# A third PSUM bank for the MLP's first layer and the dense step of a Swin-style block kernel

## The chip, the cores and the metric

The kernel runs on one core of a Trainium2 chip. The metric is the time of one execution on the device in microseconds (us); less is better. TensorE is PE in the rows (its weight loads are PEld), VectorE is DVE, ScalarE is ACT, GpSimd is POOL and SyncE, which issues most transfers, is SP.

## The reference, cut to what matters

The input is 8 images of 16 channels and 56 x 56 pixels. A depthwise 9 x 9 convolution makes 144 channels of it, which with the 16 of the input are 160 per pixel. Two Swin blocks follow, the second with windows shifted by 3 pixels, then a dense step to 144 channels, a second depthwise convolution that sums 9 channels into one, and a 1 x 1 convolution.

```python
for i, (shift, mask) in enumerate(zip(SHIFTS, (None, MASK1))):
    # inside: x = ln1(x); qkv = xw @ qkvw + qkvb; softmax(q k^T * s + bias + mask) @ v; out @ projw + projb
    #         x = sc + x; h = ln2(x); h = gelu(h @ w1 + b1) @ w2 + b2; return x + h
    x3 = _swin_block(x3, shift, mask, ln1g[i], ..., w1[i], b1[i], w2[i], b2[i])
x3 = x3 @ linw + linb
```

Windows are 7 x 7 = 49 pixels, there are 5 heads of 32, and the hidden layer of the MLP has 640 = 5 x 128 columns. Everything is in fp32; large products are made of four passes over operands that are split in a high part, a low part and a rest.

## The kernel before, in words

There are three phases. `phase_a` makes the first convolution and prepares weights, `phase_c` makes the second one. Between them, and most of the time, `phase_b` walks over 64 strips: a strip is two rows of windows' worth of tokens (14 image rows, 784 tokens, held as 7 tiles t of 112), 32 strips in layer 0 and 32 in layer 1. The loop is software-pipelined: `body(i, la, lm, ln)` holds the attention of strip i (layer `la`), the MLP of strip i-1 (layer `lm`), and the first norm, queries, keys and values of strip i+1 (`ln`). In layer 1 it also holds the dense step of strip i-1 (`linear`, with the 1 x 1 convolution folded in). Each engine has its own instruction stream, written out by hand in the order of its `body`, and waits on semaphores at constants or at values worked out from the loop variable; nothing reorders the work, so the order in the code is the order on the engine.

The eight PSUM banks of `phase_b` are: `ra` (3, a ring for all products of the attention), `so` (2, scores and outputs of heads), `rm` (2) and `pt_ps` (1). `pt_ps` holds the attention weights turned by TensorE (`weights_turned`, L1493), four times a strip, and ScalarE copies it out (`weights_out`, L1092). Between the copy of the strip's fourth group and the first group of the next strip it is empty.

The two `rm` banks are taken in strict alternation, by the class `Ring`, by these uses of a body in this order:
- G0 to G9: the first layer of the MLP, `mlp_in` (L1526). Each is one block of 128 hidden columns for the first half of the strip (G0 to G4: 4 tiles, 448 columns of tokens) or the second (G5 to G9: 3 tiles, 336 columns), and has four matmuls: z2t_hi with w_hi, z2t_lo with w_hi, z2t_hi with w_lo, z2t_rest with w_rest, all on line L127 of a helper. ScalarE empties each with a GELU into `ht` (L1119).
- W0 to W5: the second layer (`mlp_out`, L1536, matmuls on L1543), emptied by VectorE (L1323).
- in layer 1 L0 to L3: the dense step (`linear`, L1557; 2, 2, 2 and 1 tiles of four matmuls), emptied by VectorE with one L1286 per tile, in the same order.
- T2A0 and T2C0: the first half of the next strip's second norm, turned by TensorE (`mlp_turned`, L1569, transposes on L1430). ScalarE rounds them into `z2t` (L1110) and VectorE takes the low parts (`t_lo`, L1302, L1309). With that the banks are free.

On TensorE the order around them is: G0 G1 G2, the turned second half (T2A1, T2C1, into `ra`), G3 G4, scores of group 1, G5 to G9, W0, scores of group 2, `front_turned(0)` (L1448: the next strip's first norm turned, which waits for GpSimd's `z1`, L987), `weights_turned(0)`, W1, and so on; at the end of a layer 1 body values of group 2, scores of the next strip's group 0, L0 to L3, T2A0, T2C0, values of group 3, B1, and the next body's G0. G0 reads `z2t`, so it waits until VectorE's `t_lo` has freed T2C0 (`t2_half_freed`, L839).

On VectorE the end of a layer 1 body is: normalise the first half (L1205), statistics of the last tiles (L1182), the seven L1286 of L0 to L3, the variance of the second half (L1193 to L1201), `t_lo` (two L1309), normalise the second half. Each semaphore of a bank counts how often it was filled (`rm_full`) or freed (`rm_free`). With strict alternation both banks have the same number of uses in a body, 9 in layer 0 and 11 in layer 1, and `m_before` multiplies that by the bodies done.

Of the kernel before, what the change touches and what calls it, by code (L numbers as in the profile page):

```python
# [23 lines left out]
B, C, H, W = 8, 16, 56, 56  # L24
# [30 lines left out]
FT = MLP // 128  # L55
# [34 lines left out]
def reach(engine, sem, value):  # L90

    if isinstance(value, int) and value <= 0:
        return
    engine.wait_ge(sem, value)


class Ring:


    def __init__(self, uses, banks, readers):  # L100
        self.uses, self.banks = uses, banks
        self.at = {u: n for n, u in enumerate(uses)}
        self.weight = [readers.get(u, 1) for u in uses]

    def slot(self, use):
        return self.at[use] % self.banks

    def filled(self, use):
        return self.at[use] // self.banks + 1
# [7 lines left out]

    def frees(self, slot):
        return sum(self.weight[slot::self.banks])


def split_passes(nc, out, hi, lo, rest, w_hi, w_lo, w_rest, act_moves):
# [8 lines left out]
def build(nc, x, f_ana, f_syn, ln1g, ln1b, qkvw, qkvb, projw, projb, rel, ln2g, ln2b, w1, b1, w2, b2,  # L131
          linwT, linb, convwT, convb, wmask, out):
    xs0 = nc.dram_tensor("xs0", [B, H, W, DIM], F32, kind="Internal")
    xs1 = nc.dram_tensor("xs1", [B, HP, HP, DIM], F32, kind="Internal")
    ys = nc.dram_tensor("ys", [B, H, YW, DIM], F32, kind="Internal")
    relT = nc.dram_tensor("relT", [WT, 2 * HEADS * WT], F32, kind="Internal")
    with ExitStack() as ctx:
        keep = Persistent(nc, ctx)
        late = Handed(nc, ctx, xs0, ys, f_syn)
        phase_a(nc, keep, late, x, f_ana, ln1g, ln1b, qkvw, qkvb, projw, projb, rel, relT, ln2g, ln2b, w1, b1,  # L140
                w2, b2, linwT, linb, convwT, convb, wmask, xs0)
        phase_b(nc, keep, late, xs0, xs1, ys)
        late.strips.close()
        phase_c(nc, keep, late, out)
# [562 lines left out]
def phase_b(nc, keep, late, xs0, xs1, ys):  # L707
    with ExitStack() as ctx:
# [3 lines left out]
        def sem(name):  # L712
            return ctx.enter_context(nc.semaphore(name))

        def bank(name):
            return ctx.enter_context(nc.psum_tensor(name, [128, 512], F32))

        ra = [bank(f"ra{n}") for n in range(3)]
        rm = [bank(f"rm{n}") for n in range(2)]
        so = ctx.enter_context(nc.psum_tensor("so", [128, 2 * 512], F32))  # L720
        pt_ps = bank("pt_ps")
# [31 lines left out]
        s_init, s_clear = sem("b_init"), sem("b_clear")  # L753
        ra_full = [sem(f"ra_full{n}") for n in range(3)]
        ra_free = [sem(f"ra_free{n}") for n in range(3)]
        rm_full = [sem(f"rm_full{n}") for n in range(2)]
        rm_free = [sem(f"rm_free{n}") for n in range(2)]
        s_st = [sem("stats1"), sem("stats2")]
        s_rs = [sem("rs1"), sem("rs2")]
        s_pow = sem("pow2")  # L760
# [12 lines left out]
        END = Ring(["OT0", "OT1", "OT2", "OT3", "P0", "P1", "P2", "T2A1", "T2C1"], 3, {})  # L773
        PAIRS = [(0, 2), (2, 1), (3, 1), (4, 1), (5, 1), (6, 1)]
        LPAIRS = [(0, 2), (2, 2), (4, 2), (6, 1)]
        T2 = ["T2A0", "T2C0"]
        MLP_USES = [f"G{g}" for g in range(2 * FT)] + [f"W{n}" for n in range(len(PAIRS))]
        LIN_USES = ["L0", "L1", "L2", "L3"]
        RM0 = Ring(T2, 2, {})
        RM = [Ring(MLP_USES + T2, 2, {}), Ring(MLP_USES + LIN_USES + T2, 2, {})]  # L780
        RS_STEPS = [5, 3]
        PROJ = [(0, 1), (1, 3), (4, 3)]
        QH = QN // 2
# [16 lines left out]
        def a_room(i, use):  # L800
            ring = ring_a(i)
            s = ring.slot(use)
            before = 0 if ring is PRO else PRO.frees(s) + i * RA.frees(s)
            return ra_free[s], before + ring.freed_before(use)
# [7 lines left out]
        def ring_m(i, lm):  # L812

            return RM0 if lm is None else RM[lm]

        def bank_m(i, lm, use):
            return rm[ring_m(i, lm).slot(use)]

        def m_before(i, lm, per):

            if lm is None:
                return 0
            return per[0] + ((i - 1) * per[1] if lm == 0 else NS * per[1] + (i - NS - 1) * per[2])

        M_USES = [len(r.uses) // 2 for r in (RM0, *RM)]

        def m_count(i, lm, use):
            return m_before(i, lm, M_USES) + ring_m(i, lm).filled(use)

        def m_full(i, lm, use):  # L830
            return rm_full[ring_m(i, lm).slot(use)], m_count(i, lm, use)

        def m_freed(i, lm, use):
            return rm_free[ring_m(i, lm).slot(use)], m_count(i, lm, use)

        def m_room(i, lm, use):
            return rm_free[ring_m(i, lm).slot(use)], m_count(i, lm, use) - 1

        def t2_half_freed(i, lm):  # L839

            return rm_free[1], m_before(i, lm, M_USES)

        def turned_full(i, lm, use):
            return m_full(i, lm, use) if use[-1] == "0" else a_full(i, use)

        def turned_bank(i, lm, use):
            return bank_m(i, lm, use) if use[-1] == "0" else bank_a(i, use)
# [10 lines left out]
        def hi2(i, n):  # L858

            return 4 * i + n  # L860
# [181 lines left out]
        def _(act):  # L1042
            act_ = nc.scalar.activation

            def body(i, la, lm, ln):
# [59 lines left out]
                def t_hi(n, hf):  # L1105
                    t0, nt = HALF[hf]
                    for part, dst, rows in (("A", z2t[0], 128), ("C", z2t[2], CR)):
                        use = f"T2{part}{hf}"
                        act.wait_ge(*turned_full(n, lm, use))
# [67 lines left out]
        def _(dve):  # L1177
# [43 lines left out]
            def body(i, la, lm, ln):  # L1221
# [80 lines left out]
                def t_lo(n, hf):  # L1302
                    t0, nt = HALF[hf]
                    cols = slice(t0 * TT, (t0 + nt) * TT)
                    for k, (part, dst, src, rows) in enumerate((("A", z2t[1], z2t[0], slice(0, 128)),
                                                               ("C", z2t[2], z2t[2], slice(REST, 2 * REST)))):
                        use = f"T2{part}{hf}"
                        dve.wait_ge(s_hi2, hi2(n, 2 * hf + k + 1))
# [111 lines left out]
        def _(pe):  # L1420
            mm, tr = nc.tensor.matmul, nc.tensor.transpose

            def turn(z, hf, bank_of, room, full, name):
                t0, nt = HALF[hf]
                for part, f0, rows in (("A", 0, 128), ("C", 128, CR)):
                    use = f"{name}{part}{hf}"
                    reach(pe, *room(use))
                    for t in range(nt):
                        c = (t0 + t) * ZW + f0
                        last = tr(bank_of(use)[0:rows, t * TT:(t + 1) * TT], z[:, c:c + rows], keep.ident[0:TT, 0:TT])  # L1430
                    last.then_inc(full(use), 1)

            def body(i, la, lm, ln):
# [59 lines left out]
                def weights_turned(j):  # L1493
                    n = i * NG + j
                    pe.wait_ge(s_exp, n + 1)
                    reach(pe, s_pte, n)
                    for h in range(HEADS):
                        last = tr(pt_ps[:, h * GK:h * GK + QP], pr[j % 2][:, SLOT[h] * 2 * WP:(SLOT[h] + 1) * 2 * WP], gather[:])
                    last.then_inc(s_ptf, 1)
# [69 lines left out]
                def mlp_turned(n, hf):  # L1569
                    turn(z2, hf, lambda u: turned_bank(n, lm, u),  # L1570
                         lambda u: m_room(n, lm, u) if hf == 0 else a_room(n, u), lambda u: turned_full(n, lm, u)[0], "T2")

                if lm is not None:
                    pe.wait_ge(*t2_half_freed(i, lm))
                    mlp_in(range(3))
                    pe.wait_ge(s_z[1], 2 * m + 2)
                    mlp_turned(m, 1)
                    mlp_in(range(3, FT))
# [395 lines left out]
```

## Time and profile before

| what | value |
|---|---|
| time, median of 3 runs | 3090.34 us (3089.7 to 3090.7) |
| span of the profiled execution, first to last instruction | 3089.1 us |
| PE busy | 2989.3 us (97%) |
| PEld busy | 2698.0 us (87%) |
| DVE busy | 2223.4 us (72%) |
| ACT busy | 1715.3 us (56%) |
| POOL busy | 827.8 us (27%) |
| mean granted TensorE clock | 0.988 |

Times inside the profile are microseconds from the start of its span. The profiled execution is one of its own; its time outside the trace is not known beyond the span. Busy time counts an engine from the start of an instruction to its modelled end; matmuls are pipelined and overlap, so a short wait of TensorE for a bank shows as a longer first matmul and as idle time of PEld rather than as idle time of PE.

### The profile page before, as it was taken

The page shows a single profiled execution, that of the slowest core. Times are in us where ns is not written, and L with a number is a line of the kernel's source. Part 1 is how long each engine was busy: PE and PEld are TensorE (multiplying, and loading weights), DVE is VectorE, ACT ScalarE, POOL GpSimd, SP SyncE. Part 2 cuts the span into 40 slices and gives each one's busy share as a digit, 9 for nine tenths or more (in the row PEclk, how much of TensorE's full clock was granted, in tenths as well). Part 3 has the DMA queues.
Part 4 walks back from the last instruction along what each step waited for, and adds up shares of the span by engine and source line. Part 5 has one row for each costly group of instructions (what it writes and reads, how often), then busy time and mean ns, then how long its engine had stood idle before and what let it go on. Part 6 is the DMA issues. An engine that isn't in the chain of part 4 may idle for free. (4 is left out here: it accounts for less than half of the span.)

```text
span 3089.1 us, 102841 instructions
## 1 busy us (share of the span) xinstructions
PE 2989.3 (97%) x39898; PEld 2698.0 (87%) x39898; DVE 2223.4 (72%) x6736; ACT 1715.3 (56%) x4076; POOL 827.8 (27%) x1470
## 2 busy tenths in 40 slices
PE   8889999999999999999999999999999999999799
PEld 6679888898888888898888888888888889888699
DVE  5667777777777777777777777777777777777422
ACT  6456656666655656666555655565556555655321
POOL 8122222222222222222232233223322332232110
PEclk9989999999999999999999999999999999999899
DMA  6411111111111111113111111111111111112284
GB/s 142 155 60 41 38 34 39 30 35 39 39 39 39 39 33 39 31 34 93 44 39 29 33 40 33 29 37 40 33 26 40 40 33 26 40 40 42 43 141 82
DMA packets 210425, 147.29 MB, mean 48 GB/s; under 512 B 15955, under 2 KB 205206, under 8 KB 210332
## 3 DMA queue, kind: packets, MB, share of 16 engines
q1 hardware_dynamic: 207619, 142.41, 19.7%
q10 hardware_dynamic: 1008, 3.44, 0.5%
q0 software_dynamic: 1728, 0.48, 0.1%
q8 instruction: 48, 0.79, 0.1%
q14 instruction: 22, 0.17, 0.0%
HBM read 95.64 MB, written 52.50 MB: 48 GB/s over the span
## 5 line engine op out<-in xcount | busy, mean ns | idle before, releaser
L1543 PE MATMUL rm<-w,ht 128*112 128x160 f32 x4480 | 682.7, 302 | 0.0
L1543 PEld LDWEIGHTS rm<-w,ht 128*112 128x112 f32 x4480 | 611.8, 177 | 5.2
L1029 POOL TENSOR_TENSOR rs<-ln_tmp,mhalf 112x4 f32<-112x4 f32 (+1 forms) x128 | 119.1, 931 | 1625.0 <-DVE ln_tmp L1201 1624.9
L1119 ACT ACTIVATE ht<-rm 128x448 f32<-128x448 f32 (+1 forms) x640 | 319.0, 498 | 193.4 <-PE rm L127 193.4
L1084 ACT ACTIVATE vb<-ra 113x320 f32<-113x320 f32 x256 | 113.1, 442 | 278.4 <-PE ra L127 276.8
L127 PE MATMUL rm<-z2t_hi,w_hi 128*128 128x448 f32 (+1 forms) x640 | 257.2, 402 | 4.4 <-DVE z2t_rest L1309 3.3
L987 POOL TENSOR_TENSOR z<-z,one 112x448 f32<-112x448 f32 (+2 forms) x192 | 131.3, 684 | 354.9 <-DVE z L1205 354.9
L127 PE MATMUL rm<-z2t_rest,w_rest 98*128 98x448 f32 (+1 forms) x640 | 219.9, 344 | 0.0
L127 PE MATMUL rm<-z2t_lo,w_hi 128*128 128x448 f32 (+1 forms) x640 | 219.1, 342 | 0.0
L127 PE MATMUL rm<-z2t_hi,w_lo 128*128 128x448 f32 (+1 forms) x640 | 218.2, 341 | 0.0
L1248 DVE TENSOR_TENSOR sc<-so,tabs 113x490 f32<-113x490 f32 x256 | 171.3, 669 | 54.8 <-PE so L1489 42.5
L1510 PEld LDWEIGHTS so<-vb,pt 49*49 49x49 f32 x10240 | 142.6, 122 | 60.3 <-issue 55.0
L1265 DVE RECIPROCAL rd<-so 113x10 f32<-113x10 f32 x256 | 56.1, 219 | 190.7 <-PE so L1510 183.0
L1101 ACT ACTIVATE ot_hi<-ra 128x98 fp32r<-128x98 f32 x512 | 103.1, 260 | 152.5 <-PE ra L1522 151.0
L127 PEld LDWEIGHTS rm<-z2t_hi,w_hi 128*128 128x128 f32 x640 | 121.0, 189 | 73.5 <-ACT ht L1119 37.1
L1258 DVE TENSOR_TENSOR sm<-sc,mx 113x490 f32<-113x490 f32 x256 | 173.1, 676 | 13.9
L1489 PEld LDWEIGHTS so<-kt,qm 64*49 64x49 f32 x8192 | 140.9, 122 | 48.0 <-issue 42.6
L1430 PE MATMUL ra<-ident,z 112*128 112x112 f32 (+1 forms) x1280 | 164.3, 268 | 14.8 <-POOL z L987 13.8
L1060 ACT ACTIVATE qm<-ra,qpair 128x400 f32<-128x400 f32 x256 | 138.2, 591 | 69.9 <-PE ra L127 69.9
L1255 DVE TENSOR_REDUCE mx<-sc 113x10 f32<-113x490 f32 x256 | 169.2, 661 | 6.4
L1489 PE MATMUL so<-kt,qm 64*49 64x49 f32 x8192 | 172.7, 208 | 1.0 <-ACT k L1076 1.0
L1510 PE MATMUL so<-vb,pt 49*49 49x33 f32 x10240 | 170.0, 210 | 2.9 <-issue 0.9
(258 smaller groups left out, 8848.5 us busy)
## 6 DMA issues: line engine op xcount, KB each, us to landing
xa<-xs SPq DMA_DIRECT2D x128, 245.0 KB
xr<-xs SPq DMA_DIRECT2D x128, 245.0 KB
xs<-xo SPq DMA_DIRECT2D x64, 245.0 KB
ys<-yz SPq DMA_DIRECT2D x64, 245.0 KB
c_y<-ys SPq DMA_DIRECT2D x36, 260.0 KB
xs<-a_tok SPq DMA_DIRECT2D x14, 560.0 KB, 6.6
xs<-tok_late SPq DMA_DIRECT2D x14, 560.0 KB, 6.8
a_nat<-in_x ACTq DMA_DIRECT2D x7, 480.0 KB, 6.4
```

The source lines that it names most:

```text
L127: last = nc.tensor.matmul(out, lhs, rhs, start=(n == 0), stop=(n == len(pairs) - 1))
L987: gp.tensor_tensor(view(t, 0, TT, t0 * ZW + DIM, [[ZW, nt], [REST, 2], [1, REST]]), once, view(one, 0, TT, 0, [[0, nt], [0, 2], [0, REST]] ...
L1029: gp.tensor_tensor(rs[1][:, t0:t0 + nt], ln_tmp[1][5][:, t0:t0 + nt], mhalf[:, 0:nt], ALU.pow).then_inc(s_pow, 1)
L1060: last = act_(qm[:, odd * QN + hf * QH:odd * QN + (hf + 1) * QH], bank_a(i, use)[:, 0:QH], ACT.Copy, scale=keep.qpair[:, odd:odd + 1])
L1119: act_(ht[:, f * SN + t0 * TT:f * SN + (t0 + nt) * TT], bank_m(i, lm, use)[:, 0:nt * TT], ACT.Gelu_apprx_tanh).then_inc(m_freed(i, lm, use ...
L1248: v.tensor_tensor(view(sc, 0, QP, 0, [[SX, 2], [1, SX]]), view(so, 0, QP, 0, [[512, 2], [1, SX]]), tab, ALU.add).then_inc(s_sadd, 1)
L1255: v.tensor_reduce(mx[:], s3, AX.X, ALU.max).then_inc(s_smax, 1)
L1258: v.tensor_tensor(sm[j % 2][:].rearrange("q (g k) -> q g k", k=WT), s3, view(mx, 0, QP, 0, [[1, 2 * HEADS], [0, WT]]), ALU.subtract).then_ ...
L1430: last = tr(bank_of(use)[0:rows, t * TT:(t + 1) * TT], z[:, c:c + rows], keep.ident[0:TT, 0:TT])
L1489: last = mm(so[w * WP:w * WP + WT, row * 512 + b * WT:row * 512 + (b + 1) * WT], q, k, start=True, stop=True)
L1510: last = mm(so[w * WP:w * WP + WT, p * 512 + OC + h * VW:p * 512 + OC + (h + 1) * VW], pt[p * WP:p * WP + WT, h * GK + w * WT:h * GK + (w ...
L1543: last = mm(bank_m(i, lm, use)[0:TT, t * DIM:(t + 1) * DIM], ht[:, c:c + TT], keep.w["w2", lm][:, f * DIM:(f + 1) * DIM], start=(f == 0), ...
```

## The change

`pt_ps` becomes the third bank of the MLP's ring, under the name `shared = [*rm, pt_ps]` (slots 0, 1, 2). The class `Slots` replaces `Ring` for it: each use names its slot by hand. G0 to G9 go through slots 0, 1, 2 in turn, W0 to W5 alternate between slots 1 and 0 (so none lies in `pt_ps` while the attention weights go through it), L0 to L3 take 1, 0, 2, 1. T2A0 takes slot 1 in layer 0 and slot 0 in layer 1, and T2C0 takes slot 2 in both. The counts of fills per body now differ from slot to slot (7, 7, 4 in layer 0 and 9, 8, 5 in layer 1). TensorE waits once more per strip: before the first `weights_turned` it asks that G8, the last MLP use of slot 2 before it, has been emptied.

```diff
--- before.py
+++ after.py
@@ -119,6 +119,26 @@
         return sum(self.weight[slot::self.banks])
 
 
+class Slots:
+
+
+    def __init__(self, uses):
+        self.uses = [u for u, _ in uses]
+        self.of = dict(uses)
+        seen = {}
+        self.nth = {}
+        for u, s in uses:
+            seen[s] = seen.get(s, 0) + 1
+            self.nth[u] = seen[s]
+        self.total = [seen.get(s, 0) for s in range(3)]
+
+    def slot(self, use):
+        return self.of[use]
+
+    def filled(self, use):
+        return self.nth[use]
+
+
 def split_passes(nc, out, hi, lo, rest, w_hi, w_lo, w_rest, act_moves):
 
     pairs = [(hi, w_hi), (lo, w_hi), (hi, w_lo), (rest, w_rest)]
@@ -753,8 +773,9 @@
         s_init, s_clear = sem("b_init"), sem("b_clear")
         ra_full = [sem(f"ra_full{n}") for n in range(3)]
         ra_free = [sem(f"ra_free{n}") for n in range(3)]
-        rm_full = [sem(f"rm_full{n}") for n in range(2)]
-        rm_free = [sem(f"rm_free{n}") for n in range(2)]
+        rm_full = [sem(f"rm_full{n}") for n in range(3)]
+        rm_free = [sem(f"rm_free{n}") for n in range(3)]
+        shared = [*rm, pt_ps]
         s_st = [sem("stats1"), sem("stats2")]
         s_rs = [sem("rs1"), sem("rs2")]
         s_pow = sem("pow2")
@@ -773,11 +794,12 @@
         END = Ring(["OT0", "OT1", "OT2", "OT3", "P0", "P1", "P2", "T2A1", "T2C1"], 3, {})
         PAIRS = [(0, 2), (2, 1), (3, 1), (4, 1), (5, 1), (6, 1)]
         LPAIRS = [(0, 2), (2, 2), (4, 2), (6, 1)]
-        T2 = ["T2A0", "T2C0"]
-        MLP_USES = [f"G{g}" for g in range(2 * FT)] + [f"W{n}" for n in range(len(PAIRS))]
-        LIN_USES = ["L0", "L1", "L2", "L3"]
-        RM0 = Ring(T2, 2, {})
-        RM = [Ring(MLP_USES + T2, 2, {}), Ring(MLP_USES + LIN_USES + T2, 2, {})]
+        T2 = [("T2A0", 1), ("T2C0", 2)]
+        MLP_USES = [(f"G{g}", g % 3) for g in range(2 * FT)] + [(f"W{n}", (n + 1) % 2) for n in range(len(PAIRS))]
+        LIN_USES = [("L0", 1), ("L1", 0), ("L2", 2), ("L3", 1)]
+        T2_LIN = [("T2A0", 0), ("T2C0", 2)]
+        RM0 = Slots(T2)
+        RM = [Slots(MLP_USES + T2), Slots(MLP_USES + LIN_USES + T2_LIN)]
         RS_STEPS = [5, 3]
         PROJ = [(0, 1), (1, 3), (4, 3)]
         QH = QN // 2
@@ -814,18 +836,18 @@
             return RM0 if lm is None else RM[lm]
 
         def bank_m(i, lm, use):
-            return rm[ring_m(i, lm).slot(use)]
-
-        def m_before(i, lm, per):
+            return shared[ring_m(i, lm).slot(use)]
+
+        def m_before(i, lm, slot):
 
             if lm is None:
                 return 0
+            per = [r.total[slot] for r in (RM0, *RM)]
             return per[0] + ((i - 1) * per[1] if lm == 0 else NS * per[1] + (i - NS - 1) * per[2])
 
-        M_USES = [len(r.uses) // 2 for r in (RM0, *RM)]
-
         def m_count(i, lm, use):
-            return m_before(i, lm, M_USES) + ring_m(i, lm).filled(use)
+            ring = ring_m(i, lm)
+            return m_before(i, lm, ring.slot(use)) + ring.filled(use)
 
         def m_full(i, lm, use):
             return rm_full[ring_m(i, lm).slot(use)], m_count(i, lm, use)
@@ -838,7 +860,7 @@
 
         def t2_half_freed(i, lm):
 
-            return rm_free[1], m_before(i, lm, M_USES)
+            return rm_free[2], m_before(i, lm, 2)
 
         def turned_full(i, lm, use):
             return m_full(i, lm, use) if use[-1] == "0" else a_full(i, use)
@@ -1494,6 +1516,8 @@
                     n = i * NG + j
                     pe.wait_ge(s_exp, n + 1)
                     reach(pe, s_pte, n)
+                    if j == 0 and lm is not None:
+                        pe.wait_ge(*m_freed(i, lm, "G8"))
                     for h in range(HEADS):
                         last = tr(pt_ps[:, h * GK:h * GK + QP], pr[j % 2][:, SLOT[h] * 2 * WP:(SLOT[h] + 1) * 2 * WP], gather[:])
                     last.then_inc(s_ptf, 1)
```

## Rows read from the trace of the kernel before

**Rows 1.** the page, busy time of the engines, and the granted clock in 40 slices

```profile
PE 2989.3 (97%) x39898; PEld 2698.0 (87%) x39898; DVE 2223.4 (72%) x6736; ACT 1715.3 (56%) x4076; POOL 827.8 (27%) x1470
...
PEclk9989999999999999999999999999999999999899
```

**Rows 2.** waits of the whole span: us in total, times, longest

```profile
PEld so L1489 <- issue: 42.6, 192, 1.1
...
PEld rm L127 <- ACT ht L1119: 37.1, 188, 0.2
PEld rm L127 <- DVE z2t_rest L1309: 29.7, 63, 2.4
...
PE rm L127 <- DVE yz L1286: 15.1, 31, 1.8
...
PE rm L1430 <- DVE yz L1286: 11.8, 31, 0.5
```

**Rows 3.** timeline of PE, layer 0, G0 to G2: start, duration, instruction

```profile
1026.67 0.37 PE L127 MATMUL rm<-z2t_rest,w_rest 98*128 98x448 f32 x1
...
1027.08 0.36 PE L127 MATMUL rm<-z2t_lo,w_hi 128*128 128x448 f32 x1
...
1027.48 0.37 PE L127 MATMUL rm<-z2t_rest,w_rest 98*128 98x448 f32 x1
...
1027.98 0.36 PE L127 MATMUL rm<-z2t_lo,w_hi 128*128 128x448 f32 x1
```

**Rows 4.** the same, G6 to G9

```profile
1032.69 0.31 PE L127 MATMUL rm<-z2t_rest,w_rest 98*128 98x336 f32 x1
...
1033.19 0.32 PE L127 MATMUL rm<-z2t_lo,w_hi 128*128 128x336 f32 x1
...
1033.50 0.32 PE L127 MATMUL rm<-z2t_rest,w_rest 98*128 98x336 f32 x1
...
1033.81 0.31 PE L127 MATMUL rm<-z2t_lo,w_hi 128*128 128x336 f32 x1
...
1034.11 0.32 PE L127 MATMUL rm<-z2t_rest,w_rest 98*128 98x336 f32 x1
...
1034.62 0.31 PE L127 MATMUL rm<-z2t_lo,w_hi 128*128 128x336 f32 x1
```

**Rows 5.** timeline of ACT in the same strip, G5 and G9

```profile
1032.42 0.45 ACT L1119 ACTIVATE ht<-rm 128x336 f32<-128x336 f32 x1 [0.32 <-PE rm L127]
...
1035.29 0.45 ACT L1119 ACTIVATE ht<-rm 128x336 f32<-128x336 f32 x1 [0.36 <-PE rm L127]
```

**Rows 6.** timeline of DVE, end of a layer 1 body

```profile
2047.34 1.24 DVE L1286 SCALAR_TENSOR_TENSOR yz<-rm,std,yz 112x160 f32<-112x160 f32 x4
2049.11 0.97 DVE L1286 SCALAR_TENSOR_TENSOR yz<-rm,std,yz 112x160 f32<-112x160 f32 x3 [0.53 <-PE rm L127]
...
2050.80 0.16 DVE L1201 TENSOR_TENSOR ln_tmp<-ln_tmp,ln_tmp 112x3 f32<-112x3 f32 x1
2051.06 0.62 DVE L1309 TENSOR_TENSOR z2t_lo<-rm,z2t_hi 128x448 fp32r<-128x448 f32 x1
2051.72 0.62 DVE L1309 TENSOR_TENSOR z2t_rest<-rm,z2t_rest 32x448 fp32r<-32x448 f32 x1
```

**Rows 7.** timeline of PE, the same stretch

```profile
2048.05 0.33 PE L127 MATMUL rm<-lin_hi,z2t_hi 128*112 128x160 f32 x1 [0.45 <-DVE yz L1286]
...
2049.85 0.98 PE L1430 MATMUL rm<-ident,z 112*128 112x112 f32 x8 [0.38 <-DVE yz L1286]
...
2052.39 0.47 PE L127 MATMUL rm<-z2t_hi,w_hi 128*128 128x448 f32 x1
```

**Rows 8.** timeline of POOL, the same stretch

```profile
2048.72 1.55 POOL L1007 TENSOR_TENSOR x1b<-x1b,b 112x640 f32<-112x640 f32 x1
```

**Rows 9.** timeline of POOL, layer 0, before the first norm is turned

```profile
1036.85 0.93 POOL L987 TENSOR_TENSOR z<-z,one 112x448 f32<-112x448 f32 x1 [2.12 <-DVE z L1205]
```

**Rows 10.** timeline of PE, the same strip

```profile
1038.50 0.98 PE L1430 MATMUL ra<-ident,z 112*128 112x112 f32 x8
```

## The prediction

> **What bounds the kernel now.** I read the page first. It shows TensorE busy 97% of the span and the others far below, with a granted clock in its highest tenth nearly throughout, which is the 2.4 GHz level [rows 1]. So the order on PE is the path that sets the end, and there are two ways for a change of banks to gain: PE waits for a bank, or PE waits at a point whose other side a bank holds up. A change that removes neither is worth nothing. Then I read the waits, which say who waits for the ring of two banks [rows 2]. PE itself shows 15.1 + 11.8 us for VectorE's L1286, the emptying of the dense step, 31 times each. PEld shows more: 188 waits of 0.2 us each for ScalarE's GELU, and 63 waits, 29.7 us, for VectorE's low parts of T2C0 before G0. As idle time of PE the 188 don't appear at all, because the matmul before them is still ending. What they cost has to be read from the starts of matmuls in the timeline.
>
> **The GELU waits (G2, G7, G9).** From the start of a block's last matmul to the second start of the next block PE takes 0.41 us from G0 to G1 (1026.67 to 1027.08) and 0.50 us from G1 to G2 (1027.48 to 1027.98) [rows 3]. G2 wants the bank of G0, G1 that of T2C0, long free. The loss at G2 is 0.09 us. In the second half the undisturbed step is 0.31 us (G7 to G8, 1033.50 to 1033.81), while G6 to G7 takes 0.50 us and G8 to G9 takes 0.51 us: 0.19 and 0.20 us lost [rows 4]. The sum is 0.48 us a strip at three places, 0.16 us each, and 188 such waits [rows 2] are three in nearly each of the 64 strips: 188 x 0.16 = 30.1 us.
>
> Does a third bank remove all three? G2 gets slot 2, whose last user T2C0 has been freed before G0 starts, since that is what G0 waits for. G7 gets the bank of G4 in place of that of G5, G8 that of G5, G9 that of G6. In the strip shown ScalarE has emptied G5 by 1032.42 + 0.45 = 1032.87 [rows 5]. G7 starts at about 1032.85 without its stall, so G8, one block of 4 x 0.155 us later, wants slot 2 at 1033.47 and even its weight load, some 0.2 us ahead, finds it free. A block of G takes PE 0.62 us and ScalarE 0.45 us [rows 4, 5], so ScalarE doesn't fall back. W0 takes the slot of G7 and W1 that of G9, with a block and more between. T2C0 and L2 enter `pt_ps` only after the heads' fourth group was turned, copied and multiplied. I take the whole 30.1 us; the lower end, if the weight load still misses its bank once in three, is 20.
>
> Is the time kept behind W0? The next thing that doesn't move with PE is the next strip's first norm. In layer 0 GpSimd ends it at 1036.85 + 0.93 = 1037.78 [rows 9] and PE turns it from 1038.50 [rows 10]: 0.72 us of room against 0.48 us gained, 0.24 us left for the semaphore. The GELU of G9 ended at 1035.74 [rows 5], and comes earlier itself by what G7 and G9 no longer lose, so the exponentials behind it on ScalarE also move. All else up to the next G0 hangs on PE's own order and moves with it.
>
> **The end of a layer 1 body.** PE starts L2 at 2048.05 after 0.45 us of waiting for L0's bank, and T2A0 at 2049.85 after 0.38 us for L2's bank [rows 7]. After the change L2 has `pt_ps`, free, and starts at about 2047.5. L3 wants L0's bank; VectorE frees it after two of the four tiles that begin at 2047.34 [rows 6], so at 2048.0, before L3 at about 2048.3. T2A0 wants L1's bank, free when those four end, 2048.58. T2C0 wants L2's, which VectorE frees at about 2049.2. The 0.83 us of PE's waits become some 0.1 us.
>
> That is not the gain, since PE soon meets G0, which waits for VectorE. Its second L1309 ends at 2051.72 + 0.62 = 2052.34 and G0 starts at 2052.39 [rows 6, 7]. So the gain is by how much VectorE's chain moves. It runs: seven L1286 (four from 2047.34 to 2048.58, 0.53 us idle for PE's L2, three from 2049.11 to 2050.08), the variance to 2050.96, L1309 twice [rows 6]. Without the idle stretch it moves by 0.53 us; if a fifth to seventh tile adds (1.24 - 0.97) = 0.27 us each behind the four, the seven end at 2049.39 in place of 2050.08, by 0.69 us. I take 0.6 us: 31 x 0.6 = 18.6 us (16.4 to 21.4). Can others follow? PE takes at most 2052.39 - 2049.85 = 2.54 us from T2A0 to G0 [rows 7]; from 2048.7, and with 0.3 us lost at T2C0, it gets there by 2051.6, G0's new time being 2051.8. The power of the second half on GpSimd waits for that variance, at 2050.36 then, and GpSimd is free at 2048.72 + 1.55 = 2050.27 [rows 8]: 0.1 us of room. ScalarE's rounding lies between T2A0's start and the first L1309: 2051.06 - 2049.85 = 1.21 us are enough for it before, and 2050.45 - 2048.7 = 1.75 us are left then. In layer 0 there is no dense step and nothing is gained at that end. The last body has no attention to follow, and gives L2's wait, 0.45 us.
>
> **What is added.** One wait on PE before the first `weights_turned` of a strip, for G8. Queued behind it are five transposes, W1 and the outputs of group 0, and ScalarE's copy of the weights waits for them. ScalarE had emptied even G9, later in its order, by 1035.74, and PE isn't there before 1038.50 [rows 5, 10]: it is passed at once. Two waits stand there already. A wait that PE can't take in ahead costs at most 42.6 / 192 = 0.22 us by the stalls before the scores [rows 2], 63 x 0.22 = 13.9 us; below nothing it can't be. I take 0, the neighbour: G1 too begins with a wait whose bank is free, and it runs at the undisturbed pace [rows 3]. The unequal counts of the slots need other factors in the arithmetic of the waits, which I also take at 0 for the same reason. No instruction of an engine, no transfer and no queue of SP or POOL is moved; POOL and SP wait for the same events under other counts.
>
> **The sum.** 30.1 + 18.6 + 0.45 = 49.2 us. It is made on an execution whose span is 3089.1 us, 1.2 us below the median of the runs, 3090.3; that rest stays. 3090.3 - 49.2 = 3041.1 us. What a measurement can tell from no change is about 0.2%, 6 us.
>
> **A rule that speaks against it.** With rows alone the ring of two loses 0.48 us a strip, and a third bank gives it back. The Trainium skill (TensorE: Matmul & The Clock Gate, HAM oscillation — how this bites in real kernels) tells of a matmul kernel where "Adding PSUM double-buffering gave no further gain". By that the time would stay at 3090; it is the second rival below.
>
> **Rivals.**
> - G0 doesn't move. Something else on G0's path (GpSimd's power with its 0.1 us of room, ScalarE's rounding of T2C0, PE's own values and B1) holds it where it was, and of the layer 1 end only little is left: 3090.3 - 30.1 = 3060 us. For it speaks how close the three come, against it that none of them is later than VectorE by the rows. 9%.
> - The waits move instead of going. If ScalarE were the slower side of the blocks of G, more banks would only let PE run ahead once and wait as long later, and the dense step's would pass to G0: 3090 us. Against it stand 0.45 us of ScalarE against 0.62 us of PE, and its idle 0.32 and 0.36 us before G5 and G9 [rows 5]. 3%.
> - A part of the first term is lost: the first norm in layer 0 comes too late when its signal takes over 0.24 us, or G8 or W0 still miss a weight load. 20 of 30.1 us are left: 3051 us. 14%.
> - Slower: the counters. The ring's uses, 18 in a layer 0 body and 22 in a layer 1 body, 1280 in all, each wait at a value that PE's sequencer works out in the loop, now with a factor for each slot. If this no longer fits behind the running matmul, each use loses its weight load's lead, 0.09 us as at G2 [rows 3]: 1280 x 0.09 = 115 us more, 3041 + 115 = 3156 us. It decides from 49.2 / 1280 = 0.04 us a use. For it speaks only that PE has no idle time to hide it; against it that G1, G4 and G8 wait at such values now and lose nothing. 3%.
>
> **How the numbers follow.** The forecast, both terms nearly whole (3034 to 3049), has 71%, the rivals 9, 3, 14 and 3%. The predicted time is 3041. The low end: the second term at its upper value, 21.4 us, gives 3038, and if G0's wait, 29.7 / 63 = 0.47 us a time [rows 2], shrinks by a quarter in layer 0 too, 31 x 0.12 = 4 us more, 3034. The high end takes in the partly lost first term and the upper cost of the added wait (3041 + 13.9 = 3055) and the case of G0 held, 3061. Faster by over 0.2%: 94%; within 0.2%: 3%; slower: 3%.
>
> **What would show it.** Right: PEld's waits for ACT ht gone from 188 to a handful; the steps to G2, G7 and G9 at 0.41 and 0.31 us; no wait of L2 for yz; L1309 behind seven unbroken L1286; strips shorter by 0.48 us in layer 0 and 1.1 us in layer 1. G0 still waits for z2t_rest, in layer 1 with PE idle some 0.2 to 0.4 us longer. Wrong: a wait of L1430 for POOL z in layer 0 strips, idle PE before `weights_turned`, or G blocks with a step over 0.31 us though the bank was free.

## The result and the profile after

| | kernel before | changed kernel |
|---|---|---|
| time, median of 4 runs | 3090.52 us (3089.7 to 3092.99) | 3063.32 us (3060.49 to 3063.45) |
| ratio | | 0.9906, 95% interval 0.9892 to 0.992 |
| span of the profiled execution | 3089.1 us | 3059.0 us |
| strip, G0 to G0, mean of 28 in layer 0 | 40.87 us | 40.53 us |
| strip, mean of 27 in layer 1 | 44.38 us | 43.86 us |

The change saves 27 us of the 49 us that were forecast, and the time lies just above the range (3034 to 3061 us). In layer 0 a strip got 0.34 us shorter in place of 0.48 us, in layer 1 0.52 us in place of 1.08 us. The lengths of strips are the sharpest measure here: within a profile they differ by a few hundredths of a us, while the phases before and after the strips differ by some us from one execution to the next.

The waits of PE's weight loads and of PE, in the order of the whole-core list of waits (us in total, times, longest us):

```profile
PEld rm L147 <- DVE z2t_lo L1331: 38.7, 29, 1.3
...
PE rm L147 <- DVE z2t_rest L1331: 32.6, 32, 2.4
...
PEld pt_ps L1452 <- DVE yz L1308: 5.4, 29, 0.2
```

The 188 waits for the GELU [rows 2] have left the list, and so have the two of 15.1 and 11.8 us for VectorE's yz, but for one of 1.0 us. In their place PE itself waits 32.6 us at G0, in 32 strips, where 3.3 us had stood. The timeline of PE for G6 to G9 of a layer 0 strip answers to [rows 4]:

```profile
1024.25 0.32 PE L147 MATMUL rm<-z2t_rest,w_rest 98*128 98x336 f32 x1
...
1024.57 0.31 PE L147 MATMUL rm<-z2t_lo,w_hi 128*128 128x336 f32 x1
...
1025.49 0.32 PE L147 MATMUL pt_ps<-z2t_rest,w_rest 98*128 98x336 f32 x1
...
1025.81 0.31 PE L147 MATMUL rm<-z2t_lo,w_hi 128*128 128x336 f32 x1
```

G6 to G7 and G8 to G9 take 0.32 us, where they took 0.50 and 0.51 us. The end of a layer 1 body, for [rows 6 to 8]. VectorE:

```profile
1983.01 1.24 DVE L1308 SCALAR_TENSOR_TENSOR yz<-rm,std,yz 112x160 f32<-112x160 f32 x4
1984.17 0.67 DVE L1308 SCALAR_TENSOR_TENSOR yz<-pt_ps,std,yz 112x160 f32<-112x160 f32 x2
1984.75 0.38 DVE L1308 SCALAR_TENSOR_TENSOR yz<-rm,std,yz 112x160 f32<-112x160 f32 x1
1985.04 0.92 DVE L1215 TENSOR_TENSOR ln_tmp<-st 112x3 f32<-112x3 f32 x1
1985.89 0.15 DVE L1216 TENSOR_TENSOR ln_tmp<-st 112x3 f32<-112x3 f32 x1
...
1986.56 0.62 DVE L1331 TENSOR_TENSOR z2t_lo<-rm,z2t_hi 128x448 fp32r<-128x448 f32 x1
1987.21 0.62 DVE L1331 TENSOR_TENSOR z2t_rest<-pt_ps,z2t_rest 32x448 fp32r<-32x448 f32 x1
```

GpSimd and PE in the same stretch:

```profile
1984.39 1.55 POOL L1029 TENSOR_TENSOR x1b<-x1b,b 112x640 f32<-112x640 f32 x1
```

```profile
1984.31 0.60 PE L1452 MATMUL rm<-ident,z 112*128 112x112 f32 x4
...
1986.66 0.35 PE L147 MATMUL ra<-z1t_rest,qkv_rest 98*64 98x400 f32 x1
1987.96 0.47 PE L147 MATMUL rm<-z2t_hi,w_hi 128*128 128x448 f32 x1 [0.95 <-DVE z2t_rest L1331]
```

The reader is to see three things. The seven L1308 now run without a break, 2.12 us from 1983.01 to 1985.13, close to the 2.05 us that the prediction's rows give. The next operation, L1215, of 3 columns, lasts 0.92 us; it reads SBUF twice, and it ends at 1985.96, just behind GpSimd's L1029 at 1984.39 + 1.55 = 1985.94. In all 31 strips of this kind it lasts 0.90 to 0.92 us, and ends 0.02 us behind L1029 in the median. And G0 starts 0.13 us after VectorE's last L1331 (1987.83 to 1987.96), where it was 0.05 us [rows 6, 7].

### The profile page after: what moved, and what is told of

The parts are those of the page before. It is cut to its first block and busy times, and to the rows that moved or that the text cites. A ratio compares the mean times of both kernels' runs of the same rounds, so it can differ in the third digit from the quotient of the medians.

```text
span 3059.0 us, 103594 instructions
## 1 busy us (share of the span) xinstructions
PE 2954.3 (97%) x39898; PEld 2702.5 (88%) x39898; DVE 2236.5 (73%) x6736; ACT 1719.2 (56%) x4076; POOL 837.3 (27%) x1470
## 5 line engine op out<-in xcount | busy, mean ns | idle before, releaser
L1141 ACT ACTIVATE ht<-rm 128x448 f32<-128x448 f32 (+1 forms) x448 | 226.3, 505 | 146.7 <-PE rm L147 146.7
L147 PE MATMUL rm<-z2t_hi,w_hi 128*128 128x448 f32 (+1 forms) x448 | 167.4, 374 | 35.4 <-DVE z2t_rest L1331 32.6
L1522 PE MATMUL pt_ps<-gather,pr 113*128 113x113 f32 x1280 | 171.5, 265 | 0.4 <-ACT pr L1111 0.4
L1408 DVE TENSOR_TENSOR x<-ra,xr 112x480 f32<-112x480 f32 (+1 forms) x192 | 105.0, 547 | 91.3 <-PE ra L147 91.3
L147 PE MATMUL ra<-z1t_hi,qkv_hi 128*128 128x400 f32 (+1 forms) x384 | 164.4, 428 | 1.3 <-DVE z1t_rest L1253 1.1
L1116 ACT ACTIVATE pt<-pt_ps 113x490 f32<-113x490 f32 x256 | 148.5, 580 | 17.5 <-PE pt_ps L1522 13.4
```

The lines of the kernel that those rows point to most:

```text
L147: last = nc.tensor.matmul(out, lhs, rhs, start=(n == 0), stop=(n == len(pairs) - 1))
L1116: act_(pt[:], pt_ps[0:QP, 0:HEADS * GK], ACT.Copy).then_inc(s_pte, 1)
L1141: act_(ht[:, f * SN + t0 * TT:f * SN + (t0 + nt) * TT], bank_m(i, lm, use)[:, 0:nt * TT], ACT.Gelu_apprx_tanh).then_inc(m_freed(i, lm, use ...
```

## The experiments

Strip lengths are means as in the table above, taken from each run's profile. Each kernel is the changed one with the edit shown, but for e8, which edits the kernel before. The kernel before, run beside them on the same chips, had medians of 3084.84 us (e1 to e4), 3090.97 us (e5 to e8) and 3091.54 us (e9, e10). The changed kernel was not run again beside them, so a difference of a few us between its time and that of an experiment says little; the strips say it.

| run | median us | ratio to before (95%) | layer 0 strip | layer 1 strip | end of last L1331 to G0, layer 0 / 1 |
|---|---|---|---|---|---|
| before | | 1 | 40.87 | 44.38 | 0.05 / 0.05 |
| changed | 3063.32 | 0.9906 (0.9892 to 0.992) | 40.53 | 43.86 | 0.13 / 0.13 |
| e1_g_only | 3071.4 | 0.9954 (0.9937 to 0.9971) | 40.53 | 44.03 | 0.13 / 0.15 |
| e2_dense_only | 3086.86 | 1.0001 (0.9988 to 1.0014) | 40.85 | 44.27 | 0.05 / 0.13 |
| e3_swap_waits | 3059.41 | 0.9917 (0.9897 to 0.9936) | 40.44 | 43.76 | 0.06 / 0.05 |
| e4_no_b2_first | 3037.73 | 0.9848 (0.983 to 0.9866) | 40.53 | 43.10 | 0.13 / 0.13 |
| e5_write_only | 3036.66 (one run) | | 40.54 | 43.10 | 0.13 / 0.13 |
| e6_split_b2 | 3066.16 | 0.9916 (0.9898 to 0.9933) | 40.54 | 43.94 | 0.13 / 0.13 |
| e7_aggr_swap | 3014.19 | 0.9754 (0.9737 to 0.977) | 40.14 | 42.80 | 0.06 / 0.05 |
| e8_aggr_before | 3073.81 | 0.9942 (0.9925 to 0.9959) | 40.60 | 44.14 | 0.06 / 0.05 |
| e9_aggr_g_only | 3047.49 | 0.9864 (0.9835 to 0.9893) | 40.16 | 43.73 | 0.06 / 0.15 |
| e10_no_g8_wait | 3059.43 | 0.9907 (0.9877 to 0.9938) | 40.53 | 43.85 | 0.13 / 0.13 |

**e1_g_only and e2_dense_only: the two halves of the change.**

```diff
-        LIN_USES = [("L0", 1), ("L1", 0), ("L2", 2), ("L3", 1)]
-        T2_LIN = [("T2A0", 0), ("T2C0", 2)]
+        LIN_USES = [("L0", 1), ("L1", 0), ("L2", 1), ("L3", 0)]
+        T2_LIN = [("T2A0", 1), ("T2C0", 0)]
```

That is e1, and this e2:

```diff
-        T2 = [("T2A0", 1), ("T2C0", 2)]
+        T2 = [("T2A0", 0), ("T2C0", 1)]
-        MLP_USES = [(f"G{g}", g % 3) for g in range(2 * FT)] + [(f"W{n}", (n + 1) % 2) for n in range(len(PAIRS))]
+        MLP_USES = [(f"G{g}", g % 2) for g in range(2 * FT)] + [(f"W{n}", n % 2) for n in range(len(PAIRS))]
-        LIN_USES = [("L0", 1), ("L1", 0), ("L2", 2), ("L3", 1)]
-        T2_LIN = [("T2A0", 0), ("T2C0", 2)]
+        LIN_USES = [("L0", 0), ("L1", 1), ("L2", 2), ("L3", 0)]
+        T2_LIN = [("T2A0", 1), ("T2C0", 2)]
```

In both, `t2_half_freed` follows the slot of T2C0, and e2 has no wait for G8. In layer 1 of e1, T2C0 and G0 have the same slot, so that the two waits before G0 are for one event.

> The blocks of G keep their three slots; the dense step and T2 of layer 1 go back to two banks (L0 1, L1 0, L2 1, L3 0, T2A0 1, T2C0 0). Theory A (GpSimd's L1029 holds VectorE's first variance operation, so the third bank at the end of a layer 1 body gives next to nothing): strips 40.5 us in layer 0 and 43.9 to 44.0 us in layer 1, against 40.53 and 43.86 of the changed kernel, time 3063 to 3067 us. Rival B (the dense part did give its 0.6 us a strip and the blocks of G in layer 1 lost as much somewhere): layer 1 strips 44.4 us, time 3081 us.

> The other half: G and W in two banks as before, only L2 and T2C0 of layer 1 in pt_ps, no added wait. Theory A: layer 0 strips 40.87 us as before, layer 1 strips 44.3 us against 44.37, time 3086 to 3090 us, with no wait of PE for L1286's counterpart and the first variance operation of VectorE lasting until GpSimd's L1007 counterpart ends. Rival B: layer 1 strips 43.8 us, time 3072 us.

The strips say it to a few hundredths. The blocks of G give 0.34 and 0.35 us, the dense part 0.11 us in layer 1. The sum is 0.46 us; in e1 and in e2 alike G0 starts 0.08 to 0.10 us later behind L1331's counterpart than before, which both together pay once, and with that counted the two halves make up the 0.52 us to about 0.02 us. So theory A holds and B is out. Why the dense part is worth 0.18 us on top of e1 stands in a link that theory A doesn't name. In e1 VectorE's variance starts 0.6 us later in the strip than in the changed kernel and is through its first operation at the same point of it, 41.84 and 41.87 us after the strip's G0 (medians of 24 strips): that operation takes 0.29 us in place of 0.92 us. But then L1332 starts only at 42.61 us, 0.03 us behind the end of ScalarE's rounding of T2A0, where the changed kernel starts L1331 at 42.46 us, straight behind the variance. PE's wait for T2A0's bank makes that rounding late.

The time of e1, 3071 us, is above the 3063 to 3067 us that I expected. The strips of layer 1 are 0.17 us longer, 5 us in all, and the last strip 1.9 us (44.30 against 42.40 us): PE waits 1.76 us for a bank ahead of L2 there, and in the changed kernel 0.98 us ahead of L3. The profile of e1 is longer in two more places, and there the granted clock differs. The stretch ahead of the first strip, in which the kernels are the same, takes 212.9 against 207.1 us, with a granted clock of 0.62 and 0.91 in the 18 us ahead of the first G0. The first strip of layer 1 takes 45.62 against 43.77 us, with a granted clock of 0.61 (1512 to 1516 us) and 1.00 near its start.

e2 came out as expected, 44.27 us a strip in layer 1 and 3086.86 us; its interval holds no change.

**e3_swap_waits: the order of two waits.**

```diff
                 if lm is not None:
+                    room_m("G0")
                     pe.wait_ge(*t2_half_freed(i, lm))
                     mlp_in(range(3))
...
                 if lm is not None:
+                    room_m("G5")
                     pe.wait_ge(*a_freed(m, "T2A1"))
...
-                        room_m(use)
+                        if g not in (0, FT):
+                            room_m(use)
```

> The changed kernel with one order turned round: PE first waits for G0's bank and then for t2_half_freed (and for G5's bank before T2A1, T2C1), so that the arithmetic of the second value isn't between the last event and G0. Theory C (the counters differ now, so a register operation stands between the two waits at G0 and is exposed): G0's weight load starts 0.05 us after VectorE's last L1331 in place of 0.13 us, strips shorter by 0.08 us in both layers, time 3058 us. Rival D (the 0.08 us is the signal of the third bank or chance): strips unchanged, 3063 us.

Theory C holds: 0.10 us a strip in both layers, to the rounding of the table, and G0 is back at 0.05 to 0.06 us after L1331. The value of the second wait is now worked out while PE waits for the first event. With two banks of equal counts the code gives both waits at G0 the same value. Two more places bear this out: in e2, where the counts are equal in layer 0 and unequal in layer 1, G0 comes 0.05 us behind in the one and 0.13 us in the other; and in the changed kernel the five bodies that are written outside the loops, whose waits have constants, show 0.05 us (bodies 31, 32, 33, 63 and 64). The interval of the time can't tell this gain of 4 us; the strips can.

**e4_no_b2_first and e5_write_only: what holds L1215.** e4 leaves one GpSimd operation out (b2 is then missing in tiles 0 to 3 of layer 1), e5 puts a memset in its place and drops GpSimd's wait for the operation before.

```diff
-                ins = gp.tensor_tensor(part, part, view(keep.w["b2", 1], 0, TT, 0, [[0, nt], [1, DIM]]), ALU.add)
                 if hf == 1:
+                    ins = gp.tensor_tensor(part, part, view(keep.w["b2", 1], 0, TT, 0, [[0, nt], [1, DIM]]), ALU.add)
                     ins.then_inc(s_x1b, 1)
```

e5 adds to this, with `scratch` of 1280 columns:

```diff
+                else:
+                    gp.memset(scratch[:], 0.0)
```

> The changed kernel without the second GpSimd operation (L1029) of the first half of a layer 1 strip: b2 is left out of tiles 0 to 3 in layer 1. Theory A: VectorE's L1215 takes 0.3 us in place of 0.92 us, G0 comes 0.5 to 0.6 us earlier, layer 1 strips 43.3 us, time 3043 to 3048 us. Rival E (ScalarE's rounding of T2C0 or GpSimd's power is what holds VectorE's chain): L1215 short, but L1331 waits, strips 43.7 us or more, time 3058 us or more.

> The changed kernel with GpSimd's L1029 of the first half replaced by a memset of a spare tile of 1280 columns (b2 is left out of tiles 0 to 3 in layer 1). The memset runs over the same stretch and reads nothing. Theory A1 (VectorE's operation with two inputs in SBUF is held by GpSimd's reads): L1215 takes 0.15 us though the memset is still running, layer 1 strips 43.1 us as without the operation. Theory A2 (any running GpSimd instruction holds VectorE): L1215 lasts until the memset ends, 0.5 us or so, strips 43.4 us or more.

Both have layer 1 strips of 43.10 us, 0.76 us shorter; of e4 I had expected 43.3 us and 3043 to 3048 us, and it came out below both. e5 has one run alone, so what it says is in its profile. GpSimd's memset, and then VectorE's first operations of the variance in e5:

```profile
1978.87 1.17 POOL L1035 MEMSET scratch<- 112x1280 f32 x1
```

```profile
1979.66 0.15 DVE L1219 TENSOR_TENSOR ln_tmp<-st 112x3 f32<-112x3 f32 x1
1979.73 0.16 DVE L1220 TENSOR_TENSOR ln_tmp<-st 112x3 f32<-112x3 f32 x1
1979.80 0.15 DVE L1221 TENSOR_TENSOR ln_tmp<-st 112x3 f32<-112x3 f32 x1
```

The memset runs until 1980.04, over all three, and none is held. So it is not any running GpSimd instruction that holds VectorE: the memset doesn't, the addition, which reads SBUF, does. The Trainium skill says it in these words (SBUF — State Buffer, Who interferes with whom): "A DVE instruction with two SBUF inputs contends with a GpSimd instruction that reads SBUF, not with one that only writes it". The trace agrees, 0.92 us against 0.15 us. The memset and the addition differ in more than their reads, and no run here tells these differences apart.

**e6_split_b2: shorter pieces.**

```diff
-                ins = gp.tensor_tensor(part, part, view(keep.w["b2", 1], 0, TT, 0, [[0, nt], [1, DIM]]), ALU.add)
+                for t in range(t0, t0 + nt):
+                    one_t = x1b[:, t * DIM:(t + 1) * DIM]
+                    ins = gp.tensor_tensor(one_t, one_t, keep.w["b2", 1][:], ALU.add)
```

> The changed kernel with L1029 issued tile by tile, four or three operations of 160 columns in place of one of 640 or 480. Theory A: VectorE is held until the end of a piece (about 0.45 us), not of the whole, but each of its two-input operations can meet the next piece: the variance ends 0.2 to 0.4 us earlier, layer 1 strips 43.5 to 43.7 us, time 3050 to 3057 us. Rival F (GpSimd keeps its pieces back to back and VectorE gets in only behind the last): strips 43.9 us, time 3063 us or above.

A miss of theory A's numbers; the strips are those of rival F, 43.94 us, 0.08 us longer. VectorE and then GpSimd:

```profile
1991.30 0.37 DVE L1217 TENSOR_TENSOR ln_tmp<-st 112x3 f32<-112x3 f32 x1
1991.59 0.15 DVE L1218 TENSOR_TENSOR ln_tmp<-st 112x3 f32<-112x3 f32 x1
1991.66 0.49 DVE L1219 TENSOR_TENSOR ln_tmp<-st 112x3 f32<-112x3 f32 x1
1992.19 0.46 DVE L1221 TENSOR_SCALAR mean<-ln_tmp 112x3 f32<-112x3 f32 x1
```

```profile
1990.64 1.99 POOL L1031 TENSOR_TENSOR x1b<-x1b,b 112x160 f32<-112x160 f32 x4
```

VectorE does get in between the pieces, as A says, but three of its small operations are held by a piece each, the `tensor_scalar` L1221 with its one input among them, and four pieces take 1.99 us in place of 1.55 us. L1221 is let go only at 1992.65, with the last piece (until 1992.63), and the variance ends 0.08 us later than in the changed kernel.

**e7, e8 and e9: the variance without two-input reads.** `bn_aggr` makes mean and variance of a tile out of its statistics. The full edit also puts a memset of one column on VectorE ahead of them (0.06 us in the trace), and the readers of the mean take every second column.

```diff
-        mean = [sb(f"mean{n}", [TT, ST]) for n in range(2)]
+        mean = [sb("mean0", [TT, ST]), sb("mean_var", [TT, 2 * ST])]
...
-                v.tensor_tensor(total, me, mo, ALU.add)
-                v.tensor_tensor(diff, me, mo, ALU.subtract)
-                v.tensor_tensor(sq, se, so, ALU.add).then_inc(s_rs[1], 1)
+                for t in range(t0, t0 + nt):
+                    ins = v.bn_aggr(mean[1][:, 2 * t:2 * t + 2], st[1][:, t * 6:(t + 1) * 6])
+                ins.then_inc(s_rs[1], 1)
...
-                v.tensor_scalar(mean[1][:, t0:t0 + nt], total, 0.5, None, ALU.mult)
-                v.tensor_scalar(sq2, sq, 1.0 / DIM, EPS, ALU.mult, ALU.add)
-                v.scalar_tensor_tensor(hsq, diff, 0.25, diff, ALU.mult, ALU.mult).then_inc(s_rs[1], 1)
-                dve.wait_ge(s_rs[1], RS_STEPS[1] * n + 2)
-                v.tensor_tensor(var, hsq, sq2, ALU.add).then_inc(s_rs[1], 1)
+                v.tensor_scalar(ln_tmp[1][5][:, t0:t0 + nt], view(mean[1], 0, TT, 2 * t0 + 1, [[2, nt]]),
+                                EPS, None, ALU.add).then_inc(s_rs[1], 1)
```

e7 has this and the edit of e3, e9 those two and the edit of e1, e8 this alone on the kernel before.

> The changed kernel with the waits of G0 and G5 turned round, and with the variance of the second norm made of one-input operations: bn_aggr per tile and one addition of eps, in place of seven small operations of which five read SBUF twice. Theory A: nothing of GpSimd holds the variance, VectorE's chain to G0 is 1 us shorter in layer 1, until PE's own B1 bounds G0: layer 1 strips 42.8 to 43.0 us, layer 0 strips 40.2 to 40.4 us, time 3025 to 3032 us. Rival E (ScalarE's rounding of T2C0 bounds G0 soon behind): layer 1 strips 43.3 us, time 3043 us.

> The same variance in the kernel before, with its two banks. There the chain to G0 is shortened by the same operations, but L2 and T2A0 still wait for banks, and PE's idle time at G0 is only 0.42 us: layer 1 strips 44.0 to 44.1 us against 44.38, layer 0 40.7 to 40.85 us against 40.87, time 3075 to 3085 us. If it gains as much as in the changed kernel, the banks at the end of the layer 1 body were no condition of it.

> As e7 (bn_aggr, waits turned round), but with the dense step and T2 of layer 1 in two banks as in e1. It asks what the third bank is worth at the end of a layer 1 body once nothing of GpSimd holds VectorE there. Theory A (the prediction's mechanism was right and only covered): layer 1 strips 43.5 to 43.7 us, 0.7 to 0.9 us longer than the 42.80 us of e7, time 3036 to 3042 us, layer 0 unchanged at 40.15 us. Rival G (the gain of e7 is of the variance alone and would come with two banks as well): layer 1 strips 42.8 to 43.0 us, time 3014 to 3020 us.

e7 beats both kernels: 3014.19 us, 77 us below the kernel before on the same chip (ratio 0.9754, where the changed kernel had 0.9906). VectorE, GpSimd and PE at the end of a layer 1 body:

```profile
1961.22 0.18 DVE L1216 BATCH_NORM_AGGREGATE mean_var<-st 112x2 f32<-112x6 f32 x1
1961.24 0.06 DVE L1214 MEMSET dot<- 112x1 f32 x1
1961.31 0.22 DVE L1216 BATCH_NORM_AGGREGATE mean_var<-st 112x2 f32<-112x6 f32 x2
1961.56 0.36 DVE L1219 TENSOR_SCALAR ln_tmp<-mean_var 112x3 f32<-112x3 f32 x1
1961.84 0.61 DVE L1328 TENSOR_TENSOR z2t_lo<-rm,z2t_hi 128x448 fp32r<-128x448 f32 x1
```

```profile
1960.35 1.55 POOL L1030 TENSOR_TENSOR x1b<-x1b,b 112x640 f32<-112x640 f32 x1
```

```profile
1962.84 0.35 PE L147 MATMUL ra<-z1t_rest,qkv_rest 98*64 98x400 f32 x1
1963.15 0.47 PE L147 MATMUL rm<-z2t_hi,w_hi 128*128 128x448 f32 x1
```

The aggregates run beside GpSimd's operation (until 1961.90) unhindered. The addition of eps, though of one input, is still held to 1961.92. G0 starts 0.31 us after the start of PE's last own matmul, and no idle time of PE shows before it. The time is 11 us below the lower end of what I had expected, and the layer 0 strips a little too.

e9 answers the question that matters for the forecast. With the variance free, two banks at the dense step give 43.73 us and three give 42.80 us, 0.93 us a strip. Some 0.09 us of that is not the bank: in e9 T2C0 and G0 share a slot, both waits before G0 end with the same event, and G0 starts 0.15 us after L1329 in place of 0.05 us. The bank itself is worth 0.84 us, where the same edit is worth 0.18 us under GpSimd's cover (e1 against the changed kernel, 44.03 - 43.86, to rounding). Rival G is out. ScalarE and VectorE of e9 show what the second bank's lack costs:

```profile
2021.57 0.54 ACT L1134 ACTIVATE z2t_hi<-rm 128x448 fp32r<-128x448 f32 x1 [4.47 <-PE rm L1450]
```

```profile
2021.43 0.17 DVE L1220 TENSOR_SCALAR ln_tmp<-mean_var 112x3 f32<-112x3 f32 x1
2022.15 0.62 DVE L1329 TENSOR_TENSOR z2t_lo<-rm,z2t_hi 128x448 fp32r<-128x448 f32 x1 [0.54 <-ACT z2t_hi L1134]
```

VectorE is done at 2021.60 and stands idle until ScalarE has rounded T2A0 (2022.11), which PE turned late for want of the bank. The addition of eps, L1220, takes 0.17 us here, where GpSimd's addition had ended at 2021.36. From the other side: the new variance alone gives 0.24 us in layer 1 of the kernel before (e8), and 0.96 us in the changed one (e7 against e3). The two go together. In layer 0 it gives 0.27 us (e8) and 0.29 us (e7 against e3), more than expected in both. The times of e8 (3073.81 us, expected from 3075) and e9 (3047.49 us, expected up to 3042) fell outside what I had written, e8's just below and e9's above, and the layer 1 strips of both just above (44.1 and 43.7 us were the upper ends).

**e10_no_g8_wait: the added wait.**

```diff
-                    if j == 0 and lm is not None:
-                        pe.wait_ge(*m_freed(i, lm, "G8"))
```

> The changed kernel without its added wait for G8 before the first weights_turned of a strip (the exponentials that PE waits for there come after G8's GELU on ScalarE, so the order stays assured). Theory A (the wait is passed at once and costs nothing): strips 40.53 and 43.86 us as in the changed kernel, within 0.02 us, time 3063 us. Rival H (an added register wait costs PE some 0.1 us a strip): strips 40.43 and 43.76 us, time 3057 us.

The strips are the same to 0.01 us, 40.53 and 43.85. The wait is free. The median is 3059.43 us all the same, 4 us below that of the changed kernel, which shows how far two medians of different sets can be apart with equal strips.

## Why the prediction was wrong, step by step

- **The GELU waits, 0.48 us a strip.** Right in mechanism. The three stalls are gone, from G0 to the end of G9 PE gains 0.41 us in layer 0 and 0.42 us in layer 1 (mean offset of G9 from G0, before against after). About half of the 0.07 us missing stands at G5, in front of which the same arithmetic of a wait's value is exposed as at G0: with the order turned round (e3) the offset is 0.45 us. The rest is the rounding of rows to 0.01 us, of which I had added up six. 64 x 0.415 = 26.6 us in place of 30.1 us. It is kept behind W0: no new wait for GpSimd's z1 shows.
- **PE's waits for banks at L2 and T2A0.** Right: gone, and the seven operations of VectorE run unbroken.
- **The step that failed.** "Without the idle stretch it moves by 0.53 us": the chain was moved by the full gap, with the durations of its parts kept. They could not be kept. VectorE's first operation of the variance, which reads SBUF twice, was held in the kernel before already:

```profile
2050.00 0.29 DVE L1193 TENSOR_TENSOR ln_tmp<-st 112x3 f32<-112x3 f32 x1
```

It lasts 0.29 us in place of 0.15 us and ends at 2050.29, behind GpSimd's L1007 at 2050.27 [rows 8]; moving it 0.6 us ahead only made it wait 0.6 us longer. The prediction read GpSimd's end there, but only as a bound for GpSimd's own power, and called its 0.1 us of room enough. So the first rival happened, G0 nearly stayed, though by a cause that it didn't name: from the end of GpSimd's addition to G0 it is 2.12 us before and 2.02 us after. The Trainium skill (SBUF — State Buffer, Who interferes with whom) has the rule quoted at e5; the prediction did not set it against this chain.
- **A second link misread.** "1.21 us are enough for it before", is what the prediction says of ScalarE's rounding. The rows show that the rounding was the last thing that L1309 waited for. ScalarE in the kernel before, and then in the changed one:

```profile
2050.49 0.54 ACT L1110 ACTIVATE z2t_hi<-rm 128x448 fp32r<-128x448 f32 x1 [4.74 <-PE rm L1430]
```

```profile
1984.95 0.55 ACT L1132 ACTIVATE z2t_hi<-rm 128x448 fp32r<-128x448 f32 x1 [3.53 <-PE rm L1452]
```

Before, the rounding ends at 2051.03, behind the variance (2050.96), and L1309 starts at 2051.06: ScalarE, and through it PE's late T2A0, was the last to release it. After, the rounding ends at 1985.50 and the variance, at 1986.64, is last. In the medians of 24 strips L1309 starts 0.09 us behind the end of the variance before and in e1, and L1331 0.08 us ahead of its modelled end after. That is 0.17 of the 0.18 us that the dense term kept.
- **The dense term, 0.6 us a strip.** It measured 0.18 us for the changed kernel against e1, 5.6 us in place of 18.6 us. e9 against e7 shows that 0.84 us were there, more than forecast, once GpSimd doesn't stand in the way, and e4 and e5 take 0.76 us off the changed kernel by clearing GpSimd's operation.
- **The counters, taken at 0.** Wrong in size, though far from the slower rival. At G0 and G5 two waits on banks or halves stand behind each other, and the value of the second is worked out after the first is passed. e3 gives 0.10 us a strip back, in the 58 strips whose bodies are in a loop: 5.6 us. The neighbour that I argued from, G1, has one wait and shows no such cost; G0 with two was the place to look at. At all other uses of the ring it is hidden, as I had it.
- **The added wait for G8, 0.** Right (e10).

The sum with the measured terms is 26.6 + 31 x 0.18 - 58 x 0.08 = 27.5 us, against 27.2 us between the medians (0.08 us being what G0's later start costs; G5's part is in the 26.6). Of the 22 us that are missing from the forecast 49.2 us, the dense term makes 13.0 us, the counters 4.6 us and the GELU waits 3.5 us. With the dense term right the time would have lain 13 us nearer to the forecast; with the two smaller ones right, the time would still have lain inside the range.

That sum and medians agree so well is in part luck. In the two profiles the 63 strips are together 30.2 us shorter, and 2.1 and 1.9 us of it stand in two strips alone. In the first strip of layer 1 the granted clock was 0.57 from 1519 to 1523 us in the kernel before and 1.00 at the same place of the changed one (1506 to 1510 us), though PE had waited 2.0 us ahead of it in both; at 1.2 GHz in place of 2.4 GHz this cost about 1.5 us (45.88 us, where the strips behind it take 44.38 us). In the last strip PE of the kernel before waits 1.76 us for a bank ahead of L2 and 0.38 us ahead of T2A0, in the changed one 0.98 us ahead of L3, and part of the difference is the clock again (0.83 against 0.98 in the 10 us around the dense step). The body behind it, for which the prediction had 0.45 us, gains 0.15 us (from L1's last tile to L2's first it takes 0.54 us before and 0.39 us after). And the kernel before alone spreads from 3078.57 to 3097.08 us in the seven runs beside e9 and e10. What rests firmly is the strip: 0.34 and 0.52 us.

## What to carry to other kernels

When a stall on one engine is taken away, the work behind it moves to another place in time, and its durations hold only if it doesn't meet something there. Before moving a chain of VectorE ahead, look at what GpSimd does in the stretch it moves to: here an operation that reads SBUF twice waited for the end of a GpSimd operation that reads (0.92 us against 0.15 us). A small operation that ends together with a large one of the other engine is the sign of it, to be seen in the trace before. `bn_aggr` on such a path wasn't held, while `tensor_scalar` with its one input was (0.36 us against 0.17 us), so counting inputs isn't enough; cutting the other engine's operation into pieces did not help. Look also at what else ended within 0.1 us before the operation that you want to move: ahead of L1309 it was two things, the variance and ScalarE's rounding, and the change moved only one of them by much. And where two waits stand in front of one critical instruction, put the one that ends last second and have its value worked out ahead of it.

## What the runs showed that I had not expected

- GpSimd's memset of 1280 columns over the same stretch doesn't hold VectorE's two-input operations (0.15 us each), the addition of two tensors does (0.92 us).
- `bn_aggr` isn't held, a `tensor_scalar` of 3 columns with one input is: 0.36 us in e7, where, with no GpSimd operation beside it, it takes 0.17 us (e9, and layer 0 of e7), and the one of e6 takes 0.46 us.
- The work that two banks hold up need not be the waiting engine's own: PE's wait for T2A0's bank reached G0 through ScalarE's rounding (0.54 us of idle VectorE in e9).
- Register arithmetic between two waits costs 0.08 us where it is exposed, and nothing where it isn't.
